# The last state's part of y is added by TensorE while it turns y, and the shared expert's products stand in another order

## What is computed

```python
def step(h, inp):
    dA_t, Bu_t, C_t = inp
    h = dA_t * h + Bu_t
    y = jnp.sum(h * C_t[:, None, :], axis=-1)
    return (h, y)
...
return y + x * D_param
...
h = jax.nn.silu(x @ wg) * (x @ wu) / SCALING
return h @ wd
...
h = x + attention(rmsnorm(x, ln1_w), kv_d_w, q_d_w, k_u_w, v_u_w, q_u_w, rope_k_w, rope_q_w, o_w)
out = h + moe(rmsnorm(h, ln2_w), sh_gate, sh_up, sh_down, r_gate, r_up, r_down, router_w, router_b)
```

## Time and profile before

| | us |
|---|---|
| median of 3 runs | 2104.68 (2101.46 to 2108.03) |
| profiled execution, its own time | 2103.13 |
| its span, first to last instruction | 2100.9 |
| TensorE busy | 1868.6 (89%) |
| DVE busy | 1375.5 (65%) |
| POOL busy | 788.5 (38%) |
| mean granted clock of TensorE | 0.934 |

### The profile page before, as it was taken

The page is one execution under the profiler, slowest core; times in us unless marked ns, Lnnn a source line. Parts: engine busy times, 40 slices in busy tenths (PEclk is TensorE's granted clock), DMA queues, the critical chain, the costliest instruction groups (busy, mean ns, idle before and its releaser), DMA issues. The chain is left out here.

```text
span 2100.9 us, 27324 instructions
## 1 busy us (share of the span) xinstructions
PE 1868.6 (89%) x9162; PEld 1223.6 (58%) x9162; DVE 1375.5 (65%) x2196; ACT 993.6 (47%) x1738; POOL 788.5 (38%) x1057
## 2 busy tenths in 40 slices
PE   7978665998999899898999899899899899899695
PEld 3446443695448555595447656597347666588342
DVE  5765699474663699576654599677654599667311
ACT  1412674463322697363232598264242498365031
POOL 1146276541220277471120167472110157472201
PEclk9989755998999999999999999999999999999898
DMA  6337200000213176210113067210022157310683
GB/s 254 119 107 228 81 0 21 1 2 1 100 46 121 39 250 207 95 32 21 59 72 119 32 230 246 90 42 21 33 98 90 56 195 263 113 41 22 264 291 105
DMA packets 55065, 221.05 MB, mean 105 GB/s; under 512 B 6289, under 2 KB 6289, under 8 KB 46993
## 3 DMA queue, kind: packets, MB, share of 16 engines
q1 hardware_dynamic: 45776, 195.19, 26.8%
q0 software_dynamic: 5120, 16.78, 2.4%
q10 hardware_dynamic: 4032, 7.34, 1.0%
HBM read 179.70 MB, written 39.58 MB: 104 GB/s over the span
## 5 line engine op out<-in xcount | busy, mean ns | idle before, releaser
L1969 POOL TENSOR_TENSOR Y<-Y,HC 128x1024 f32<-128x1024 f32 x116 | 273.8, 2361 | 174.9 <-DVE HC L1362 174.2
L1351 DVE TENSOR_TENSOR_SCAN HS<-DA,ps 128x1024 f32<-128x1024 f32 x128 | 292.4, 2284 | 24.2 <-PE ps L747 13.5
L1720 ACT ACTIVATE DA<-DL,AB,AN 128x511 f32<-128x511 f32 x256 | 193.9, 807 | 14.8 <-DVE HS L1351 13.5
L979 PE MATMUL ps<-ring,XBT 128*128 128x512 f32 x384 | 188.1, 596 | 0.0
L1837 ACT ACTIVATE PD<-ps,NMX 128x128 f32<-128x128 f32 (+3 forms) x256 | 135.1, 530 | 101.1 <-DVE NMX L1496 98.9
L537 PE MATMUL ps<-ring,XNT 128*128 128x512 f32 x384 | 176.4, 616 | 6.5 <-ACT VA L1667 4.3
L1496 DVE TENSOR_REDUCE NMX<-ps 128x1 f32<-128x128 f32 (+3 forms) x256 | 124.2, 486 | 62.4 <-PE ps L815 61.9
L833 PE MATMUL ps<-V,PTD 128*128 128x33 f32 x1280 | 164.2, 262 | 0.0
L833 PEld LDWEIGHTS ps<-V,PTD 128*128 128x128 f32 x1280 | 162.6, 192 | 0.5 <-ACT PTD L857 0.5
L655 PE MATMUL ps<-XNH,tern 128*128 128x512 f32 x352 | 139.6, 397 | 9.2 <-DVE tern L1251 5.5
L1362 DVE TENSOR_TENSOR HC<-HS,ps 128x1024 f32<-128x1024 f32 x120 | 143.2, 1196 | 0.0
(11 more groups left out here) (251 smaller groups left out, 4000.6 us busy)
## 6 DMA issues: line engine op xcount, KB each, us to landing
ring<-experts_dram SPq DMA_DIRECT2D x48, 1024.0 KB, 5.3
tern<-tern_q SPq DMA_DIRECT2D x33, 768.0 KB, 4.3
ring<-experts_dram SPq DMA_DIRECT2D x48, 512.0 KB, 5.5
RAW<-tern_dram SPq DMA_DIRECT2D x22, 768.0 KB, 4.8
ring<-wqkv_dram SPq DMA_DIRECT2D x4, 3072.0 KB, 11.9
XB<-xg SPq DMA_DIRECT2D x42, 256.0 KB, 3.8
yg<-YB SPq DMA_DIRECT2D x42, 256.0 KB, 5.0
tern_q<-tern SPq DMA_DIRECT2D x11, 768.0 KB, 6.8
```

The costliest lines, as they stand in the source:

```text
L979: last = pe.matmul(ps[:, g_bank(b)], XBT[:, b % 2, k], weights(b)[:, k * C:(k + 1) * C], start=(k == 0), stop=(k == NK - 1), skip_group_ch ...
L1351: v.tensor_tensor_scan(HS[:, q].rearrange("p j t -> p (j t)"), DA[:, q].rearrange("p j t -> p (j t)"), ps[:, 2 * q:2 * q + 2].rearrange("p ...
L1720: s.activation(DA[:, u % 2, jj, 1:T], DL[:, j, 1:T], ACT.Exp, scale=AN[:, j * NS + n:j * NS + n + 1], bias=AB[:, j * NS + n:j * NS + n + 1 ...
L1969: p.tensor_tensor(y, y, HC[:, q], ALU.add).then_inc(c_y, 1)
```

## The change

- `v_C_end` no longer adds the last half (L1449 and `c_yt` are gone), and POOL stops one half earlier (28 sums a step instead of 29), so `HC[:, 0]` and `HC[:, 1]` of the last state stay out of `Y`.
- `pe_C_out` turns y by products with the identity instead of transposes: for each group of 128 channels one product with the `Y` tile opens the PSUM sum, and one with the `HC` tile adds to it and closes it. Per token tile that is eight products where there were four transposes.
- TensorE's order behind the scan in the steps with experts: expert pair 2, turns 0 and 1, expert pair 3, turns 2 and 3, normalized tiles 0 and 1, expert pair 0, normalized tiles 2 and 3, expert pair 1. Before: turns 0 to 3, pair 0, tile 0, pair 1, tile 1, pair 2, tiles 2 and 3, pair 3. `v_E_acc` follows the new order of pairs.
- y's first product waits for 28 sums of POOL, `c_xy` and the last `c_hc`.

```diff
         def pe_C_out(pe, experts):
-            pe.wait_ge(c_y, 2 * NS - 3)
-            pe.wait_ge(c_yt, 1)
-            for i in range(NT):
+
+            if experts:
+
+                pe.wait_ge(m_ht, NB)
+                pe_E_down(pe, 2)
+            pe.wait_ge(c_y, 2 * NS - 4)
+            pe.wait_ge(c_xy, 2)
+            pe.wait_ge(c_hc, 2 * NS)
+            def expert(i):
+                if experts:
+                    pe_E_down(pe, i)
+
+            def turn(i):
                 bank = t_bank(pe, ("y", i))
                 for j in range(NK):
-                    last = pe.transpose(ps[:, bank, tile(j)], Y[:, j, tile(i)], ident)
+                    pe.matmul(ps[:, bank, tile(j)], Y[:, j, tile(i)], ident, start=True, stop=False,
+                              skip_group_check=True)
+                    last = pe.matmul(ps[:, bank, tile(j)], HC[:, j // 2, j % 2, tile(i)], ident, start=False, stop=True,
+                                     skip_group_check=True)
                 last.then_inc(t_full, 1)
+
+            turn(0)
+            turn(1)
+            expert(3)
+            turn(2)
+            turn(3)
+            pe_norm(pe, 3, 0)
+            pe_norm(pe, 3, 1)
+            expert(0)
+            pe_norm(pe, 3, 2)
+            pe_norm(pe, 3, 3)
             if experts:
-                pe.wait_ge(c_hc, 2 * NS)
                 pe.wait_ge(m_y, NB)
-                pe.wait_ge(m_ht, NB)
-                pe_E_down(pe, 0)
-            for i in range(NT):
-                pe_norm(pe, 3, i)
-                if experts and i != 2:
-                    pe_E_down(pe, i + 1 if i < 2 else i)
+            expert(1)
...
-        def v_E_acc(v, i):
-            v.wait_ge(e_down, i + 1)
+        def v_E_acc(v, n, i):
+            v.wait_ge(e_down, n + 1)
...
         def v_C_end(v, experts):
-            v.wait_ge(c_hc, 2 * NS)
-            v.wait_ge(c_y, 2 * NS - 4)
-            v.tensor_tensor(Y[:, 2:4], Y[:, 2:4], HC[:, 1], ALU.add).then_inc(c_yt, 1)
...
-                for i in range(NT):
-                    v_E_acc(v, i)
+                for n, i in enumerate((2, 3, 0, 1)):
+                    v_E_acc(v, n, i)
...
-            for u in range(2, 2 * NS - 1):
+            for u in range(2, 2 * NS - 2):
```

More of the change, by code:

```diff
@@ L427, in build @@
         c_xy = sem("c_xy")
-        c_yt = sem("c_yt")
         e_logit = sem("e_logit")
@@ L1439, in v_experts @@
             for i in range(NT):
-                v_E_acc(v, i)
+                v_E_acc(v, i, i)
             for b in range(NB):
```

## The result

| | before | changed |
|---|---|---|
| median, us | 2104.68 (17 runs) | 2098.98 (17 runs, 2094.55 to 2105.25) |
| profiled execution | 2103.13 | 2098.14 |
| its span | 2100.9 | 2096.2 |
| mean granted clock | 0.934 | 0.943 |

The ratio is 0.9972, 95% interval 0.9962 to 0.9982: 5.7 us less. That is 0.28%, just inside what I had called no change, and beyond its interval.

What follows compares the result with a forecast made beforehand. TensorE is busy 89%, but DVE and POOL bind step 1 between scan and L773, and TensorE is last in expert steps; +1.2 - 1.3 - 1.3 + 1.0 = -0.4 us, set against the median as 2104.3 us, range 2098.5 to 2110.

Steps and rivals of the forecast that it cites:

- no change: Whole kernel: differences within about 0.3%, 6.3 us, cannot be told apart; chance of such a result 0.78.
- the first rival: All steps: TensorE's clock stays up, also into step 1's L773; -5.7 us, 2099.0; 16 in 100.
- The first step: Scan end to L773, step 1: cold turns of y delay the X sums, L773 as cold as before; 1.2 us lost.
- An expert step at 2.4 GHz: Scan end to L773: X's head start is spent, one pair fewer stands behind DVE; 1.3 us won.
- An expert step whose clock falls before y: Scan end to L773: the cold expert pair ahead of y is a new wait; 1.0 us lost, assumed in one step.
- The second rival: Turns of y stay at 1.2 GHz in all steps; +14.1 us, 2118.8; 10 in 100.
- Four records a product: Turns of y: each product runs four records, 3.46 us a turn; +23.5 us, 2128.2; 2 in 100.
- my price: Turns of y: two records per fp32 product, 0.108 us apart at 2.4 GHz, so 1.73 us a turn.
- a step lost its gain again between L773 and the barrier: Behind the changed stretch: a stated sign of error, the step's 1.3 us being lost again there.
- two chances in a hundred: Another stage that the shift touches changes the time, in either direction; 2 in 100, no size given.

Runs made afterwards that it cites:

- the products alone: Kernel before with y turned by products that add the last state's part, last DVE and POOL sums gone, expert pairs in the old order: 0.9990, -2.1 us.
- the first step alone: Kernel before with y turned by the new products in step 1 only, expert steps and their order as before: ratio 0.9980, -4.2 us.
- the order alone: Kernel before with only the new order of expert pairs, y still turned by transposes after DVE's sum: ratio 1.0001, run again 0.9993.
- the expert steps alone: Kernel before with the whole change in the three expert steps only, step 1 as before: ratio 0.9992, -1.7 us.
- pair 3 late: Changed kernel with expert pair 3 moved from between turns 1 and 2 to behind turn 3: ratio 0.9973 against the kernel before, -5.7 us.

## Why the prediction was right, and where it was not

The range (2098.5 to 2110) held the time by half a microsecond. The forecast, 2104.3, was that of the wrong case: the measured 2098.98 is that of the first rival, *the clock holds everywhere* (2099.0, 16 in 100), and even that sum is right by two errors that cancel: it has 3.9 us from the expert steps, where the run with these alone gave 1.7, and 1.75 from the first step, where the run with that alone gave 4.2.

*The first step* is the step that failed. I let the clock rise 5.5 us into the products, taken from L773 in the earlier trace rows, and fall back ahead of D. (By the records it rose 6.1 us into L773; 377 was the end of my window.) It rose 3.2 us into them, and in the changed kernel and the products alone it stood until D. The slow records were also 0.213 us apart and not 0.23. So the term was -2.9 us, not +1.2. What I had right is that D starts no earlier (S + 14.73 for S + 14.58) and that X sums come later. The fall that I assumed does occur, in the profiled run of the first step alone. Of the term's two outcomes (-1.7 by the rival, +1.2) I took the worse as the likely one, on one stretch of the last step; the time of that edit alone, -4.2 (-7.2 to -1.5), speaks for the better one as the common one, and so do four of five profiled executions. That the range held is luck as far as this term goes: its sign was wrong.

*An expert step at 2.4 GHz*: mechanism right, size off, -0.8 for -1.3. The head start of X is spent behind pair 3, the gain appears because one pair fewer stands behind DVE's chain, and L790 comes at S + 15.27 where I had S + 14.8. Mis-sized were the records' distance, 0.112 us for 0.108 (48 of them, 0.2 us), and the head: y stands 0.26 us behind S where I had 0.06, with no part of the pair in it, since it is 0.26 in the first step too. What I did not see is that the order alone wins more there, 1.7 us a step, and that the products give back 0.9 of it.

*An expert step whose clock falls before y*: one of three again, the second, and it lost 0.6 where I had 1.0. The pair in front of y is a new wait there, as described, of 1.5 us where I had 2.5. That it was one of three again is luck: with the expert steps alone it was none, with pair 3 late two.

*The second rival* (turns at 1.2 GHz) is out: the records are 0.112 apart in all expert steps. *Four records a product* too: the 9354 records against 9162 are 48 more in each of four steps, so two for each of the 32 products. The page "FP8 and Floating Point Precision" of the Trainium skill, section TensorE Precision Notes, has four passes for true fp32. That need not mean four records: each record took 0.43 us for 512 columns, two cycles of 2.4 GHz a column, so two records are four cycles a column. I was wrong to read the page as speaking against my price.

*Outside the sum*: I wrote that I would be wrong if a step lost its gain again between L773 and the barrier. In the order alone that is what happened, and in the changed kernel's second step. I had no term for it but two chances in a hundred. Nor had I one for the kernel's last stretch, which won 2.8 us in this execution.

What stays open: whether falls of the clock at the end of D and at the head of the attention come more often with a new order. The counts behind the table (11 of 24 expert steps against 1 of 15 at the end of D) speak for it, but not for the changed kernel itself (1 of 9), and steps of one execution are not independent, with one profiled execution per kernel. Why the clock falls in one of these steps and not in the next is open too.

## What to carry to other kernels

Before costing a change in a stretch, read TensorE's granted clock in that stretch and in the next: here the largest term was not a wait but the clock at which the 16 product records behind it ran, and three unused products in an idle stretch did, by the medians, two thirds of the real change (-3.8 us, interval -6.7 to -0.8). Work moved into an engine's idle time ahead of a dependency is worth its full length only if the engine is the last one behind it; read who is last at the join (here TensorE in front of D, not DVE), and how many of the moved pieces still stand behind. And where the clock can fall in other places, take the time from many runs and the mechanism from the stretch, since a few microseconds won in a profiled stretch and the span of the same execution may have opposite signs.

## What the runs showed of the hardware

- A product of fp32 with the identity, 128 by 128, is two records 0.112 us apart, 0.22 us for what a transpose does in one record of about 0.11; two of them that add in PSUM take the place of a transpose and of a sum beforehand. Here 32 products a step (7.2 us of TensorE at full clock) stood in for 16 transposes (1.8 us), a DVE sum of 1024 columns (2.34 us) and one on POOL (2.35 us).
- In the first step the clock stood at 0.50 through 12 transposes with TensorE busy 2.94 of 3.00 us; with products at the same place it rose after 3.2 us. Whether it is the form or the length of the row that does it, no run shows: with one product for each transpose it rose 4.7 us behind y's start, and the transposes are over after 4.5.
- The clock fell in stretches that the change does not touch, in some executions and not in others: at the head of the attention (1531 to 1538 in the kernel with pair 3 late) and behind the 33-column products at the end of D. Such a fall at the end of D cost 1.1 to 1.9 us, one at the head of the attention 2.9. All outside the four stretches took between 2001 and 2012 us in thirteen profiled executions.
